# A decoder layer with a quantised feed-forward part: the down weights' rounding in single passes, two raw buffers, the running maximum two half chunks later

## The reference, cut to what matters

```python
def fake_quant(t, axis):
    s = jnp.max(jnp.abs(t), axis=axis, keepdims=True) / QMAX
    s = jnp.maximum(s, 1e-08)
    q = jnp.clip(jnp.round(t / s), -QMAX - 1.0, QMAX) * s
    return t + jax.lax.stop_gradient(q - t)

def qlinear(x, w):
    return jnp.einsum('bsh,oh->bso', fake_quant(x, -1), fake_quant(w, 1))

gate = qlinear(x, w_gate)
up = qlinear(x, w_up)
h = jax.nn.silu(gate) * up
return qlinear(h, w_down)
```

## Time and profile before

| What | us |
|---|---|
| Three runs | 1761.95, 1765.27, 1769.07 |
| Median | 1765.27 |
| Profiled execution | 1760.79 |
| Its span | 1759.0 |
| VectorE busy over the span | 1368.5 (78%) |
| TensorE busy over the span | 1399.6 (80%) |
| ScalarE busy over the span | 911.5 (52%) |
| GpSimd busy over the span | 970.8 (55%) |
| Stage of the gate and up products, TensorE's first to its last | 1429.6 to 1632.8 |
| First matmul of the down product | 1662.7 |

### The profile page before, as it was taken

The page is one execution under the profiler, slowest core; times in us unless marked ns, Lnnn a source line. Parts: engine busy times, 40 slices in busy tenths (PEclk is TensorE's granted clock), DMA queues, the critical chain, the costliest instruction groups (busy, mean ns, idle before and its releaser), DMA issues. The chain is left out here.

```text
span 1759.0 us, 17587 instructions
## 1 busy us (share of the span) xinstructions
PE 1399.6 (80%) x5358; PEld 714.0 (41%) x5384; DVE 1368.5 (78%) x1642; ACT 911.5 (52%) x1314; POOL 970.8 (55%) x794
## 2 busy tenths in 40 slices
PE   6998578778778967578787887788999778787478
PEld 3443344444434434344444444444444333333333
DVE  6675798998998999999988989991584647575684
ACT  1212667667667657677667577551422233534550
POOL 0000878788788778899889888971000002222350
PEclk9999788898999988769999999999999979988799
DMA  7694343443443432434845736734821146663204
GB/s 279 215 355 183 108 126 114 148 138 114 148 138 114 140 123 72 151 115 133 273 168 210 220 127 220 235 150 167 314 81 49 52 110 148 129 125 101 54 0 168
DMA packets 155466, 264.36 MB, mean 150 GB/s; under 512 B 76560, under 2 KB 94096, under 8 KB 149552
## 3 DMA queue, kind: packets, MB, share of 16 engines
q1 hardware_dynamic: 151056, 236.27, 41.7%
q10 hardware_dynamic: 4320, 27.00, 4.4%
HBM read 207.60 MB, written 38.60 MB: 140 GB/s over the span
## 5 line engine op out<-in xcount | busy, mean ns | idle before, releaser
L1031 DVE TENSOR_TENSOR_SCAN hbuf<-decay,hbuf 128x512 f32<-128x512 f32 x512 | 612.1, 1212 | 48.6 <-ACT decay L757 48.6
L577 PE MATMUL turn<-ident,hbuf 128*128 128x128 f32 x2048 | 348.0, 301 | 209.6 <-DVE hbuf L1031 167.0
L757 ACT ACTIVATE decay<-delta,chan_sb 128x512 f32<-128x512 f32 x512 | 348.5, 687 | 318.8 <-DVE hbuf L1031 317.7
L577 PEld LDWEIGHTS turn<-ident,hbuf 128*128 128x128 f32 x2048 | 263.5, 154 | 489.2 <-DVE hbuf L1031 244.5
L1045 DVE SCALAR_TENSOR_TENSOR acc<-turn,pn,acc 128x512 f32<-128x512 f32 x360 | 263.4, 732 | 30.3 <-PE turn L577 28.7
L868 POOL TENSOR_TENSOR hbuf<-du,sx 128x512 f32<-128x512 f32 x172 | 213.0, 1272 | 1.9 <-DMA sx<-bt_scratch 1.9
L868 POOL TENSOR_TENSOR hbuf<-wout,sx 128x512 f32<-128x512 f32 x172 | 213.4, 1277 | 0.4 <-POOL wout L878 0.2
L1716 PE MATMUL bank<-codes,wout 128*128 128x512 bf16 (+1 forms) x690 | 166.7, 403 | 37.5 <-DVE gs L1868 35.8
L889 POOL TENSOR_TENSOR acc<-acc,part 128x512 f32<-128x512 f32 x120 | 153.6, 1280 | 58.1 <-ACT part L767 57.1
L1833 POOL TENSOR_TENSOR hid<-gs,us 128x512 f32<-128x512 f32 (+1 forms) x44 | 55.9, 1271 | 159.6 <-ACT gs L1784 159.6
L559 PE MATMUL bank_g<-wout,codes 128*128 128x512 f32 x256 | 138.0, 626 | 1.0 <-DVE wout L968 1.0
(11 more groups left out here) (206 smaller groups left out, 2116.0 us busy)
## 6 DMA issues: line engine op xcount, KB each, us to landing
wout<-in_woutT SPq DMA_DIRECT2D x48, 512.0 KB, 4.2
sx<-bt_scratch SPq DMA_DIRECT2D x86, 256.0 KB, 3.7
codes<-in_wg SPq DMA_DIRECT2D x8, 2048.0 KB, 8.8
ubuf<-u_scratch SPq DMA_DIRECT2D x16, 1024.0 KB, 5.8
wout<-in_w_gate SPq DMA_DIRECT2D x26, 512.0 KB, 4.6
wout<-in_w_up SPq DMA_DIRECT2D x26, 512.0 KB, 4.2
raw_d<-in_w_down ACTq DMA_DIRECT2D x8, 1376.0 KB, 7.1
b_more<-bt_scratch SPq DMA_DIRECT2D x42, 256.0 KB, 3.4
```

Source lines behind the costliest of these rows:

```text
L577: last = pe.transpose(turn[t % 2][:, j * P:j * P + P], hbuf[:, s % 4, j, t * P:t * P + P], ident[:, :])
L757: act.activation(decay_bank[q % 2][:, :], delta[:, G % 2, j, :], ACT.Exp, scale=a_col(GD * (G % GROUPS) + j, n)).then_inc(dA_done, 1)
L1031: dve.tensor_tensor_scan(h, decay_bank[q % 2][:, :], h, 0.0, ALU.mult, ALU.add).then_inc(scan_done, 1)
```

## The change

The table `wd_at` is gone. All loops of the stage now run over half chunks `k` from 0 to 43. The 48 rounding passes (8 tiles, 3 pieces, 2 passes) are handed out over the 38 half chunks from 5 on, one or two in each, between the silu of half chunk k and the size of half chunk k-1. `raw_d` has two buffers. `us` has three (`UR`), two of them in a row of `wout` that the fourth weight buffer held; `WT` goes from 4 to 3. The running maximum of half chunk k-2 stands behind the two scalings of half chunk k, and the gate scaling of k waits for the product of k-2 alone. The product of k gets a wait for the maximum of k-2. SyncE transposes a tile of codes in the half chunk after its last pass. Some small tables move into spare rows, with their sizes rounded up and their use unchanged.

```diff
-WT = 4
+WT = 3
...
+    UR = 3
+    SLOTS = BATCH * OC
...
-        raw_d = sb("raw_d", [P, INTER])
+        raw_d = sb("raw_d", [P, 2, INTER])
...
-        us = sb("us", [P, 2, L])
+        us_own = sb("us", [P, L])
+        us_row = keep.wout[:, OC // 2 + WT, :].rearrange("p (a t) -> p a t", t=L)
+        us = [us_own[:, :], us_row[:, 0, :], us_row[:, 1, :]]
...
-        wd_at = {c: t for t, c in enumerate((0, 3, 6, 9, 12, 15, 18, 21))}
+        WD_FIRST, WD_SLOTS = 5, 38
+
+        def wd_pieces(k):
+            q = 2 * NP * JT
+            i = k - WD_FIRST
+            return range(q * i // WD_SLOTS, q * (i + 1) // WD_SLOTS) if 0 <= i < WD_SLOTS else range(0)
+
+        def wd_first(k):
+            return [q // (2 * NP) for q in wd_pieces(k) if q % (2 * NP) == 0]
+
+        def wd_last(k):
+            return [q // (2 * NP) for q in wd_pieces(k) if q % (2 * NP) == 2 * NP - 1]
...
-            for c in range(OC):
-                if c + WT < OC:
-                    load_wT(c + WT)
-                if c - 2 in wd_at:
-                    turn_wd(wd_at[c - 2])
-            turn_wd(JT - 1)
+            for k in range(SLOTS):
+                if k % BATCH == 0 and k // BATCH + WT < OC:
+                    load_wT(k // BATCH + WT)
+                for t in wd_last(k - 1):
+                    turn_wd(t)
...
             def load_wd(t):
-                if t >= 1:
-                    act.wait_ge(wd_plain, NP * t)
-                act.dma_start(raw_d[:, :], w_down[t * P:t * P + P, :]).then_inc(wd_load, 16)
+                if t >= 2:
+                    act.wait_ge(wd_plain, NP * (t - 1))
+                act.dma_start(raw_d[:, t % 2, :], w_down[t * P:t * P + P, :]).then_inc(wd_load[t % 2], 16)
...
+            for k in range(SLOTS + 1):
+                if k < SLOTS:
+                    silu(k)
+                for q in wd_pieces(k):
+                    t, m = q // (2 * NP), q % (2 * NP)
+                    if m < NP:
+                        codes_d(t, m)
+                    else:
+                        plain_d(t, m - NP)
+                if k >= 1:
+                    size(k - 1)
+                for t in wd_last(k):
+                    if t + 2 < JT:
+                        load_wd(t + 2)
...
+                pool.wait_ge(gate_silu, k + 1)
+                pool.wait_ge(up_scaled, k + 1)
+                if k >= 2:
+                    pool.wait_ge(peak_done, k - 1)
...
-                dve.wait_ge(gate_mm, 2 * c + b + 1)
-                if c >= 1:
-                    dve.wait_ge(hid_done, 2 * (c - 1) + b + 1)
-                    dve.wait_ge(peak_done, 2 * (c - 1) + b + 1)
+                dve.wait_ge(gate_mm, k + 1)
+                if k >= 2:
+                    dve.wait_ge(hid_done, k - 1)
...
+                dve.wait_ge(up_mm, k + 1)
+                if k >= UR:
+                    dve.wait_ge(peak_done, k - UR + 1)
...
+            for k in range(SLOTS + 2):
+                if k < SLOTS:
+                    scale_products(k)
+                if k >= 2:
+                    raise_peak(k - 2)
+                for t in wd_first(k + 2):
+                    scales_d(t)
```

More of the change, by code:

```diff
@@ L1626, in feed_forward @@
         wT_load = [sem(f"wT_load{i}") for i in range(WT)]
-        wd_load = sem("wd_load")
+        wd_load = [sem(f"wd_load{i}") for i in range(2)]
         x2_load = [sem(f"x2_load{i}") for i in range(2)]
@@ L1656, in feed_forward, with at @@
         block = ctx.enter_context(nc.Block())
-        wd_at = {c: t for t, c in enumerate((0, 3, 6, 9, 12, 15, 18, 21))}
+        WD_FIRST, WD_SLOTS = 5, 38
[7 more added lines that the diff above has]
+            return [q // (2 * NP) for q in wd_pieces(k) if q % (2 * NP) == 2 * NP - 1]
+        def at(k):
+            c, b = k // BATCH, k % BATCH
+            return c, b, rows(c)
         def piece(m):
@@ L1778, in plain_d, with silu @@
                     act.wait_ge(wd_turned, 16 * t)
-                act.activation(code_d[:, piece(m)], raw_d[:, piece(m)], ACT.Identity, bias=rnd[:, 1:2]).then_inc(wd_plain, 1)
-            def silu(c, b):
-                r = rows(c)
-                act.wait_ge(gate_scaled, 2 * c + b + 1)
+                act.activation(code_d[:, piece(m)], raw_d[:, t % 2, piece(m)], ACT.Identity, bias=rnd[:, 1:2])\
+                    .then_inc(wd_plain, 1)
+            def silu(k):
+                c, b, r = at(k)
+                act.wait_ge(gate_scaled, k + 1)
@@ L1784, in silu, with size @@
                 act.activation(gs[0:r, b, :], gs[0:r, b, :], ACT.Silu).then_inc(gate_silu, 1)
-            def size(c, b):
-                r = rows(c)
-                act.wait_ge(hid_done, 2 * c + b + 1)
-                act.activation(us[0:r, b, :], hid[0:r, c, b * L:b * L + L], ACT.Abs).then_inc(size_done, 1)
+            def size(k):
+                c, b, r = at(k)
+                act.wait_ge(hid_done, k + 1)
+                act.activation(us[k % UR][0:r, :], hid[0:r, c, b * L:b * L + L], ACT.Abs).then_inc(size_done, 1)
@@ L1791, in load_wd @@
             def load_wd(t):
-                if t >= 1:
-                    act.wait_ge(wd_plain, NP * t)
-                act.dma_start(raw_d[:, :], w_down[t * P:t * P + P, :]).then_inc(wd_load, 16)
-            load_wd(0)
-            act.wait_ge(const, 3)
-            for c in range(OC + 2):
-                for b in range(BATCH):
-                    if c >= 2:
-                        size(c - 2, b)
-                    if 1 <= c <= OC:
-                        silu(c - 1, b)
-                if c - 1 in wd_at:
-                    t = wd_at[c - 1]
-                    for m in range(NP):
-                        codes_d(t, m)
-                    for m in range(NP):
-                        plain_d(t, m)
-                    if t + 1 < JT:
-                        load_wd(t + 1)
+                if t >= 2:
+                    act.wait_ge(wd_plain, NP * (t - 1))
@@ new lines, in load_wd @@
+                act.dma_start(raw_d[:, t % 2, :], w_down[t * P:t * P + P, :]).then_inc(wd_load[t % 2], 16)
+            for t in range(2):
+                load_wd(t)
+            act.wait_ge(const, 3)
+            for k in range(SLOTS + 1):
[4 more added lines that the diff above has]
+                    if m < NP:
+                        codes_d(t, m)
+                    else:
[5 more added lines that the diff above has]
+                        load_wd(t + 2)
@@ L1840, in _ @@
             pool.memset(code_d[:, INTER:OC * P], 0.0).then_inc(pad_made, 1)
-            for c in range(OC + 1):
-                if c >= 1:
-                    for b in range(BATCH):
-                        multiply(c - 1, b, rows(c - 1))
+            for k in range(SLOTS):
+                multiply(k)
             pool.wait_ge(ih_kept, 2)
@@ L1885, in _ @@
             dve.wait_ge(const, 3)
-            for c in range(OC + 2):
-                for b in range(BATCH):
-                    if c >= 2:
-                        raise_peak(c - 2, b)
-                    if 1 <= c <= OC:
-                        scale_products(c - 1, b)
-                if c in wd_at:
-                    scales_d(wd_at[c])
+            for k in range(SLOTS + 2):
+                if k < SLOTS:
+                    scale_products(k)
+                if k >= 2:
+                    raise_peak(k - 2)
+                for t in wd_first(k + 2):
+                    scales_d(t)
             dve.wait_ge(peak_turned, 1)
@@ L1946, in __init__ @@
         self.yT = codes_space[:, :].rearrange("p (w c t) -> p w c t", w=2, t=P)
-        self.late = wout[:, OC // 2:OC // 2 + 4, :]
+        self.late = wout[:, OC // 2:OC // 2 + WT, :]
         self.wT = self.late.rearrange("p i j -> p (i j)").bitcast(BF16).rearrange("p (i m k r) -> p i m k r", m=2, k=KC, r=P)
```

49 lines of the change are left out of this document (21 added, 28 removed).

## The result

The changed kernel takes **1698.3 us** in the median (1696.6 to 1702.31, 4 runs) against 1763.61 for the kernel before on the same chip. The ratio is 0.9627, interval 0.9600 to 0.9654: faster by 3.7%, 65 us. The forecast was 1700 in a range of 1690 to 1722.

A forecast was written before the change was run, and what follows sets the result against it. With the ring of waits cut, TensorE was to bound the stage: 1583.5 + 4.9 + 107.4 = 1695.8, less 1 for the clock; 1696.8 for the profiled execution, 1701 with 0.25% added, said as 1700, range 1690 to 1722.

The forecast's parts named there:

- The bound now: Gate and up stage before: waits among gate scaling, silu, size and maximum go round in 3.50 us per half chunk.
- TensorE's own time: Gate and up products: without waits TensorE needs 6.91 us per chunk, 3.45 per half chunk, so it ends at 1583.5.
- rival C: TensorE's clock falls from cycling through banks: each of 21 chunks loses 2.3 us, 1748; chance 2%.
- VectorE and ScalarE under 3.45 per half chunk: Gate and up stage: VectorE needs 2.8 us and ScalarE 2.55 per half chunk, both under TensorE's 3.45.
- ScalarE's stalls: ScalarE's plain pass waits 3.9 us for the transpose of the tile before; cost 0 while the reserve holds.
- Rival E: Weights come too late for three buffers behind a long codes transpose; slower, 1774 at 22 us; chance 3%.
- Three weight buffers: Weight loads: even behind a 9.31 us hold of SyncE's queue they land 2.7 before needed; cost 0.
- The second raw buffer: Raw loads of down tiles: 14 us from load to reduction against 8.5 needed; worth 0.
- The end: From TensorE's last product to the peak transposes: 4.9 us, set by TensorE's 16 matmuls that spread the down scales.
- Rivals A and B: A: ScalarE's reserve does not hold, 1716, chance 15%. B: codes transposes form a ring, 19.4 per tile, 1732, 4%.
- the reserve of six half chunks: A ScalarE stall reaches TensorE only over six half chunks, 20 us, later; ScalarE wins back 0.9 per half chunk.
- E's formula: A codes transpose holding SyncE's queue x us makes TensorE wait x - 9.3 - 2.7, plus 2.3 of clock, at six tiles.

The follow-up runs named there:

- the run with the old order: Changed kernel with the running maximum ahead of the scalings on VectorE again and the gate scaling waiting for it, passes still spread: 1732.93 us.
- the run with both undone: Changed kernel with the maximum ahead of the scalings again and the six rounding passes of a tile in one go: 1757.19 us.
- the run with thirds: Changed kernel with each third of a tile of codes transposed by its own transfer, in the half chunk after its plain pass: 1717.74 us.

## Why the prediction was right

- **The number.** The sum gave 1696.8 for the profiled execution, which took 1702.31, 5.5 more: the first product came 3.6 later, the end took 1.2 more, and the 1 us allowed for the clock did not come. The 0.25% put on top, which I called partly chance, covers 3 of these, and the median lies 4 under the profiled execution. So that 1700 falls within 2 of 1698.3 is in part luck; the length of the stage, forecast at 158.8 (to 1583.5 + 4.9 from 1429.6) and measured at 160.0, is not.
- **The bound now.** "The ring, not TensorE, sets it": shown, by the run with the old order (1732.9) and by the run with both undone (1757.2).
- **TensorE's own time.** 21 chunks of 6.91 behind chunk 0 were to make 153.9 from the first product; measured 153.90. The clock stayed at 1.00 over 145 us in spite of a bank change every 8 matmuls, so rival C is out for a TensorE that doesn't stop between its groups; one that does isn't tested here.
- **VectorE and ScalarE under 3.45 per half chunk.** Held. That the product's wait keeps maximum and product apart was the reason given for a short maximum, and it was wrong: without the wait the maximum is as short, and the product takes the loss. It changed nothing in the sum.
- **ScalarE's stalls.** 3.9 each was worked out for two of them; there are six, 26.5 in all, 4.4 in the mean, and TensorE has no wait behind them. The terms under that were off. The first transpose, without a raw load beside it, landed after 5.3 (I took 5.5). The last two had none beside them either, and took 5.2. The five between took 8.8 to 10.9, where I took 8 for the one that I worked out. The late passes bring the raw load next to the transpose, since one follows the last pass and the other waits for it: the load at 1492.78 and the transpose at 1493.74, then both at 1529.2, both at 1542.7. Rival E's "raw loads now mostly run before" was wrong.
- **Three weight buffers.** A reserve of 2.7 in the worst case, cost 0. The cost was 0 in one profile and 0.49 in the other, but the worst case was set too low: loads of weights took up to 13.0 and transposes up to 14.2 in the same kernel, for which the row before allowed 4.8 and 11.2. Two buffers cost 6 to 7 us over three, so three do have a margin over two; how much is left of it in the worst case is not known.
- **The second raw buffer.** I put it at 0. It is worth some 7 us where the passes stand in one go; for spread passes it wasn't tried.
- **The end.** 4.9 forecast, 6.1 measured. The step left out ScalarE: it took the maximum of half chunk 41 to be done at +1.6, but the last two plain passes stand in half chunk 42, ahead of the size of 41, and end at +2.0. The chain of waits there:

```profile
1587.24 1.81 ACT code_d L1794 x2
1589.05 0.53 ACT wout L1805
1589.60 0.70 DVE wout L1899
...
1590.46 1.27 POOL hid L1853
...
1592.42 0.69 DVE wout L1899
...
1593.16 1.62 PE bank L1746 x8
```

  The product of half chunk 43 (1590.46) waited for the maximum of 41 (1589.60) that waited for that size (1589.05), the wait which the change put on GpSimd. Without that wait the end was no shorter (7.7 in its profile), and in the second profile of the changed kernel it was 7.0, so it also moves with how far ScalarE is behind. The higher clock that I allowed 1 for is seen on the scale and peak matmuls (2.02 for 16, 1.61 for 8) but was behind the chain or given back by the next 16 (3.78).
- **The rest.** 107.4 from the peak transposes to the end was forecast unchanged; it is 1700.5 - 1593.2 = 107.3.

Rivals A and B needed the reserve of six half chunks to run out. It didn't at 8 matmuls per product; at 7 TensorE waited for the gate scaling once for 0.5 and once for 3.5, so that bound is near; whether it is A's or B's was not separated.

Rival E's mechanism is real. In the run with thirds a transpose held the queue for 17.1 us and TensorE waited 9.3; E's formula gives 17.1 - 9.3 - 2.7 = 5.1. It has only the queue in it. The two weight loads behind the transpose were slow as well, 6.8 to issue (1493.35) where the sum had 2.6, and that is the 4.2 that it lacks. In the run with both undone the queue was held for 18.3, but TensorE's 6.9 was for weights issued ahead of the transpose, which took 19.4 to land: a way that the formula doesn't have at all. The argument against E, that raw loads now mostly run before the transposes, points the wrong way: five of the changed kernel's eight transposes had one beside them, and a raw load just ahead of a transpose is where the slow cases were seen (below). In the two profiles of the changed kernel the queue was held for 8.7 and 11.9 at most. That it was no more is timing which the prediction didn't work out, and how often it is more is not known.

## What to carry to other kernels

Where one engine has several instructions per step and a ring of waits passes through two engines, put the one that nobody needs soon (here a running maximum) behind the ones that feed the bound engine, and let it lag by two steps; that, with the third buffer it needs, gave 51 of the 59 us that order and spreading gave together. Compare the free-running pace of the bound engine, read from a stretch in which it doesn't wait, with the round of the ring, and reckon the end behind the last step by itself: together they gave a stage shorter by 63 us, and it was 62. After that the time is set by one engine, and finer schedules of the others (thirds, earlier passes) only move transfers, for better or worse.

## What the runs showed of the hardware that was not expected

- A transposing transfer of codes (a whole tile, issued from SyncE) took 5.2 to 6.0 us to land where no raw load was beside it. With a raw load of 1376 KB issued from ScalarE at the same moment or less than 0.6 us ahead of a transposing transfer, which the 14 profiles have 48 times, the raw load took 8.5 at most to land, and one issue held SyncE's queue for 9.8 at most.
- Five raw loads took far more: 11.3, 12.2, 13.0, 18.6 and 23.4, with transposes beside them of 13.3 to 24.3. All five had been issued 0.6 to 1.1 us ahead of a transposing transfer. Four others at that distance took 6.8 to 7.2, so the distance goes with it and doesn't decide it; what does is open.
- While that lasts, the queue which issues the transposes stands (17.1 and 18.3 us for one issue), so every later load in it is late as well, and so is a load of weights issued just ahead (19.4 us where 3.5 is the median before).
- A VectorE maximum of two SBUF operands and a GpSimd product that overlap lengthen only the one that starts second. Apart they take 0.69 and 1.27. In the kernel before, the maximum started 0.4 behind the product and took 1.40, the product 1.27. In the run without GpSimd's wait, a product that started 0.2 behind a maximum took 1.59, the maximum 0.68.
